# A transformer layer with routed experts on one Trainium2 core: opening turned in f32, and twelve more chunks of probabilities turned by DMA

## The reference, cut to what matters

```python
x = L0_attn_x                              # (2, 2048, 256) f32
xn = _layernorm(x, axis=-1)
# attention, one head, no key projection
scores = einsum('bqe,bke->bqk', xn @ W_qk, xn) / sqrt(256)
scores += (kpos - qpos) * alibi_slope[0]   # then the causal mask
s = einsum('bqk,bkd->bqd', softmax(scores), xn @ W_v.T)
# 8 experts, top-1 routing, capacity 512 tokens each
probs = softmax(xn @ Wr); eidx = argmax(probs)
h = maximum(xe @ W1, 0.0); ye = (h @ W2) * p_tok
x = x + s * silu(scatter(ye))
```

## Time and profile before

| what | value |
|---|---|
| median of 3 runs | 441.39 us (440.22 to 441.7) |
| the profiled execution | 440.56 us, of it 438.8 us span |
| PE busy | 420.2 us (96%) |
| DVE busy | 323.6 us (74%) |
| ACT busy | 221.7 us (51%) |
| POOL busy | 231.0 us (53%) |
| chain that ended last | PE 73%, DVE 13%, DMA 5%, ACT 4% |

### The profile page before, as it was taken

How to read it: one execution, slowest core, us unless ns; L and a number is a source line. 1 busy time by engine, 2 the same in 40 slices (tenths; PEclk the granted TensorE clock), 3 DMA queues, 4 the chain that set the end, 5 groups by cost and what they waited for, 6 DMA issues and landing times.

```text
span 438.8 us, 8377 instructions
## 1 busy us (share of the span) xinstructions
PE 420.2 (96%) x3022; PEld 287.7 (66%) x3022; DVE 323.6 (74%) x839; ACT 221.7 (51%) x436; POOL 231.0 (53%) x360
## 2 busy tenths in 40 slices
PE   5799899997999899999999999999999999999996
PEld 2367576675678677676766666666666666665676
DVE  5989778988898568778758797979696966424563
ACT  1756365353655246645435554545454545454551
POOL 5337870834726735146202666575757575757530
PEclk9999999999999999999999999999999999999999
DMA  7992749465955643266746577676778773244850
GB/s 235 357 374 68 218 133 226 94 127 109 298 149 98 103 165 71 77 229 170 143 48 253 183 232 240 196 261 184 264 174 266 178 202 92 93 119 115 154 104 30
DMA packets 99928, 74.96 MB, mean 171 GB/s; under 512 B 68911, under 2 KB 93756, under 8 KB 97840
## 3 DMA queue, kind: packets, MB, share of 16 engines
q1 hardware_dynamic: 88624, 52.06, 45.6%
q0 software_dynamic: 5824, 16.74, 12.7%
q10 hardware_dynamic: 5440, 5.64, 4.0%
HBM read 31.33 MB, written 28.58 MB: 137 GB/s over the span
## 4 chain that ended last, share of the span: by engine, by line
PE 73%; DVE 13%; DMA 5%; ACT 4%; issue 3%; POOL 0%; another core or an unknown queue 0%; ACTq 0%; SPq 0%; DVEq 0%
PE bank L1350 19%; PE bank L1352 19%; PE bank L1351 19%; PE bank L1439 4%; PE bank L1442 4%; PE bank L1441 4%; DMA pT<-p_rows 4%; DVE sc L975 3%; PE bank L1420 3%; DVE p_rows L996 2%; ACT sc L1224 2%; DVE stats L823 1%; DMA xg<-in_x 1%; DVE pT L996 1%; DVE w_l L1047 1%
## 5 line engine op out<-in xcount | busy, mean ns | idle before, releaser
L1439 PE MATMUL bank<-v_h,pT 128*128 128x257 f16 x272 | 74.6, 274 | 3.3 <-DMA pT<-p_rows 3.2
L1442 PE MATMUL bank<-v_h,pT 128*128 128x257 f16 x272 | 74.1, 272 | 0.0
L1441 PE MATMUL bank<-v_l,pT 128*128 128x256 f16 x272 | 73.7, 271 | 0.0
L1251 ACT ACTIVATE hid_h<-bank 128x512 f16<-128x512 f32 x64 | 38.0, 594 | 67.2 <-PE bank L1352 61.3
L1065 DVE SCALAR_TENSOR_TENSOR hid_l<-bank,hid_h 128x512 f16<-128x512 f32 x64 | 43.9, 685 | 37.8 <-ACT hid_h L1251 35.4
L1351 PE MATMUL bank<-w_l,hid_h 128*128 128x256 f16 x256 | 69.8, 273 | 0.0
L1350 PE MATMUL bank<-w_h,hid_h 128*128 128x256 f16 x256 | 69.8, 273 | 0.0
L1352 PE MATMUL bank<-w_h,hid_l 128*128 128x256 f16 x256 | 69.8, 273 | 0.0
L975 DVE CUSTOM_DVE_ANT_0 sc<-bank,bias,score_mul 128x512 f32<-128x512 f32 (+2 forms) x80 | 52.9, 664 | 9.6 <-PE bank L1352 9.3
L1350 PE MATMUL bank<-xT,qT_h 128*128 128x512 f16 (+3 forms) x160 | 55.0, 347 | 2.7 <-DVE cmin L975 2.4
L1351 PE MATMUL bank<-xT,qT_h 128*128 128x512 f16 (+3 forms) x160 | 55.1, 347 | 0.0
(11 more groups left out here) (183 smaller groups left out, 917.1 us busy)
## 6 DMA issues: line engine op xcount, KB each, us to landing
raw<-in_w_e SPq DMA_DIRECT2D x5, 2048.0 KB
sc<-in_w_e SPq DMA_DIRECT2D x3, 2048.0 KB
slots<-empty ACTq DMA_DIRECT2D x1, 4224.0 KB, 20.1
gates<-gate SPq DMA_DIRECT2D x8, 512.0 KB
out<-xg SPq DMA_DIRECT2D x7, 512.0 KB
rows<-xg SPq DMA_DIRECT2D x7, 512.0 KB, 7.0
rows<-so SPq DMA_DIRECT2D x7, 512.0 KB
xg<-in_x SPq DMA_DIRECT2D x6, 512.0 KB, 4.9
```

The lines of the kernel that those rows point to most:

```text
L1251: a_.activation(hid_h[:, f % HB, :], sc_ps[f % 2][:, :], ACT.Relu).then_inc(h_hi, 1)
L1439: pe.matmul(pv_ps[t % 2][:, 0:D + 1], p_h, v_h[:, at, q, 0:D + 1], start=kb == 0, stop=False)
L1441: pe.matmul(pv_ps[t % 2][:, 0:D], p_h, v_l[:, at, q, :], start=False, stop=False)
L1442: last = pe.matmul(pv_ps[t % 2][:, 0:D + 1], p_l, v_h[:, at, q, 0:D + 1], start=False, stop=kb == t % NT)
```

## The change

1. The opening. The norms of groups 0 and 1 are turned by PE in f32 (8 transposes for a group), and the split into halves is made while ACT and DVE read the bank (turned_high, turned_low). The rows that POOL scatters are gotten back from xT by four DMA transposes for a group (rows_of). Group 0's inverse deviation is made by a root on ACT, a reciprocal and a refinement on DVE; half of group 1's statistics is made on ACT.
2. Loads. `slots <- empty` (4.2 MB, ACT's queue) is issued later in the opening, the first expert's weights at t = 5.
3. by_dma is true for 12 more chunks: the first of tiles 4 to 7; (20, 0), (21, 0), (22, 0), (23, 0), (23, 1), (27, 0), (31, 0) and (31, 1). There are three buffers of rows (the third lies in hid_h, which the experts use), and a semaphore for each chunk place.
4. turn(4) goes from t = 10 to 11, turn(5) from 14 to 15.

The pieces stand in the order by_dma, buffers, SP, DVE's opening, ACT's opening, PE.

```diff
         def by_dma(t, c):
-            if t in (REST - 1, TILES - 1):
+            if chunk_blocks(t, c) < GT:
                 return False
-            if chunks(t) == 4:
-                return c == 1 if t == NT - 1 else c in ((1, 2) if t < NT else (0, 1, 2))
-            return chunks(t) == 3 and c < 2
+            if t < NT:
+                return c == 1 if t == NT - 1 else c in {2: (0,), 3: (0, 1), 4: (1, 2)}.get(chunks(t), ())
+            return c in {REST - 1: (0,), TILES - 1: (0, 1)}.get(t, range(chunks(t)) if t >= NT + GT else ())
...
+        TURN_TILE = {2: 3, 3: 6, 4: 11, 5: 15, 6: 15, LATE: REST - 8}
...
-        p_rows = [sb(f"p_rows{k}", [P, GT, 2, P], F16) for k in range(2)]
+        p_rows = [sb(f"p_rows{k}", [P, GT, 2, P], F16) for k in range(NX - 1)]
+        p_rows += [hid_h[:, HB - 2:HB, :].rearrange("p f t -> p (f t)").rearrange("p (b h t) -> p b h t", b=GT, h=2)]
...
+            def rows_of(g):
+                sp.wait_ge(xT_lo, 2 * g + 2)
+                for j in range(GT):
+                    sp.dma_start_transpose(halves[g][:, j, :].rearrange("p (b d) -> p b d", d=P),
+                                           xT[:, g, j, :, :].rearrange("p b t -> p (b t)")).then_inc(rows_back[g], 16)
...
             group_in(0)
-            sp.dma_start(raw[:, :, :], w_k[0]).then_inc(w_in[1], 16)
+            rows_of(0)
...
+                if t == 1:
+                    rows_of(1)
+                if t == 5:
+                    sp.dma_start(raw[:, :, :], w_k[0]).then_inc(w_in[1], 16)
...
-                for n in (*SPLIT_TILE, LATE):
-                    if t == {5: 14, LATE: REST - 8}.get(n, SPLIT_TILE.get(n)):
+                for n in TURN_TILE:
+                    if t == TURN_TILE[n]:
                         turn(n)
...
+            def turned_low(g, h):
+                dve.wait_ge(xT_hi, 2 * g + h + 1)
+                hi, lo = tile_rows(g, h)
+                v.scalar_tensor_tensor(lo, turned_tiles(h), X_UP, hi, ALU.mult, ALU.subtract).then_inc(xT_lo, 1)
...
-            split(0)
             query_weights()
-            rear(0)
-            norm_stats(1, range(2, GT))
-            norm_var(1)
+            turned_low(0, 0)
+            turned_low(0, 1)
...
             value_weights()
             unit(0, QRY)
+            for j in range(GT):
+                normed(1, j)
             unit(0, QRY + 1)
-            for j in range(GT - 1):
-                normed(1, j)
-            split(1)
             unit(0, VAL)
+            turned_low(1, 0)
+            dve.wait_ge(masked, 1)
+            score(0, 0)
...
+            a_.activation(warm[:, 4:5], empty[:, 0:1], ACT.Sqrt)
+            roots(0)
+            mean(2)
+            square(2)
             act.wait_ge(small_scaled, 1)
             a_.activation(wqk_h[:, :, :], wsmall[:, 0], ACT.Copy, scale=small_up[:, 0:1]).then_inc(small_hi, 1)
-            split(0)
...
             unit(0, QRY + 1)
+            a_.activation(warm[:, 4:5], empty[:, 0:1], ACT.Exp)
             unit(0, VAL)
-            split(1)
+            turned_high(1, 0)
...
             def values(t, c):
                 if by_dma(t, c):
-                    i = dma_no(t, c)
-                    pe.wait_ge(pT_in[i % 2], i // 2 * 16 + 16)
+                    pe.wait_ge(pT_in[t % 2][c], landed(t, c))
...
-                        last = pe.transpose(x_ps[h][:, at:at + P], halves[g][:, j, b * P:(b + 1) * P], ident_h[:, :])
+                        last = pe.transpose(x_ps[h][:, at:at + P], xn[:, 2 * h + j, d * P:(d + 1) * P], ident[:, :])
```

More of the change, by code:

```diff
@@ L221, in layer_kernel @@
                 [xg[j // 2].rearrange("p g d -> p (g d)")[:, j % 2 * 2 * D:(j % 2 + 1) * 2 * D] for j in range(SJ)]]
-        p_rows = [sb(f"p_rows{k}", [P, GT, 2, P], F16) for k in range(2)]
-        warm = sb("warm", [P, 4])
+        p_rows = [sb(f"p_rows{k}", [P, GT, 2, P], F16) for k in range(NX - 1)]
+        p_rows += [hid_h[:, HB - 2:HB, :].rearrange("p f t -> p (f t)").rearrange("p (b h t) -> p b h t", b=GT, h=2)]
+        warm = sb("warm", [P, 5])
+        root = sb("root", [P, GT])
+        seed = [sb(f"seed{k}", [P, GT]) for k in range(2)]
+        seed_sq = sb("seed_sq", [P, GT])
+        seed_sqv = sb("seed_sqv", [P, GT])
         bank = [ctx.enter_context(nc.psum_tensor(f"bank{k}", [P, 512], F32)) for k in range(8)]
@@ L227, in layer_kernel @@
         small_turn, small_back = bank[1][0:3, 0:P], bank[6][:, 0:3]
-        x_ps = [pv_ps[h][:, :].bitcast(F16) for h in range(2)]
+        x_ps = pv_ps
         w_turn, w_back = aux[0][0:2, 0:P], aux[1][:, 0:2]
@@ L273, in layer_kernel @@
         x_turned = sem("x_turned")
-        xT_front = sem("xT_front")
-        xT_rear = sem("xT_rear")
+        root_made = sem("root_made")
+        seed_made = sem("seed_made")
+        mean_made = sem("mean_made")
+        square_made = sem("square_made")
+        xT_hi = sem("xT_hi")
+        xT_lo = sem("xT_lo")
+        rows_back = [sem(f"rows_back{k}") for k in range(2)]
         xn_hi = sem("xn_hi")
@@ L296, in layer_kernel @@
         pT_lo = sem("pT_lo")
-        pT_in = [sem(f"pT_in{k}") for k in range(2)]
+        pT_in = [[sem(f"pT_in{k}_{c}") for c in range(NG)] for k in range(2)]
         pv_full = sem("pv_full")
@@ L367, in dma_no, with landed @@
             return chunk_no(t, c) - turn_no(t, c)
+        in_rows = [(t, c) for t in range(TILES) for c in range(chunks(t)) if by_dma(t, c)]
+        def landed(t, c):
+            return sum(by_dma(k, c) for k in range(t % 2, t + 1, 2)) * 16
         def chunk_cols(t, c):
@@ L448, in piece, with var_to, tile_rows, turned_tiles @@
             return q // PIECES, slice(q % PIECES * PIECE, (q % PIECES + 1) * PIECE)
[L450 to L457, removed]
+        def var_to(g):
+            return 1 if g == 0 else g + 2
+        def tile_rows(g, h):
+            return xT[:, g, 2 * h:2 * h + 2, 0:KD, :], xT[:, g, 2 * h:2 * h + 2, KD:2 * KD, :]
+        def turned_tiles(h):
+            return x_ps[h][:, :].rearrange("p (j k t) -> p j k t", j=2, k=KD)
+        def made_to(g):
+            return g * GT + GT if g < 2 else GT + GT + g - 1
+        def rows_to(g):
+            return g - 1
         def turned_to(g):
@@ L1372, in unit @@
                     cols = slice((n - QRY) * P, (n - QRY + 1) * P)
-                    for d in range(KD):
-                        last = product(a[:, :], wqk_h[:, d, cols], wqk_l[:, d, cols],
-                                       xT[:, at, :, d, :], xT[:, at, :, KD + d, :], d == 0, d == KD - 1)
+                    for j in [slice(0, 2), slice(2, GT)] if g == 0 else [slice(0, GT)]:
+                        if g == 0 and j.start:
+                            pe.wait_ge(xT_lo, 2)
+                        for d in range(KD):
+                            last = product(a[:, j.start * P:j.stop * P], wqk_h[:, d, cols], wqk_l[:, d, cols],
+                                           xT[:, at, j, d, :], xT[:, at, j, KD + d, :], d == 0, d == KD - 1, True)
                 elif n < RANK:
@@ L1515, in _ @@
             unit(0, VAL)
-            score(0, 0)
-            unit(0, VAL + 1)
             turn_x(1, 0)
             turn_x(1, 1)
+            unit(0, VAL + 1)
+            score(0, 0)
             unit(0, VAL + 2)
```

210 lines of the change are left out of this document (114 added, 96 removed).

## The result

| | median of the runs | profiled execution | span | mean granted clock |
|---|---|---|---|---|
| before | 441.54 us (4 runs, 440.22 to 442.42) | 440.56 us | 438.8 us | 1.0 |
| after | 475.37 us (4 runs, 472.65 to 476.26) | 476.20 us | 474.3 us | 0.964 |

The changed kernel is slower: ratio 1.0756, 95% interval 1.0726 to 1.0786. The forecast was 455, with 443 to 463 as its range. The direction was right; the loss is 34 us where 14 were expected, and 475.4 lies outside the range.

The account below looks back on a forecast made before the run. The prediction took PE, busy 96% of the span, as the bound. Terms of 12.2 us back and 27.1 lost put 440.56 + 14.9 at 455.5, stated as 455 us, range 443 to 463.

Parts of the forecast that it names:

- Transposes off PE: Added DMA chunks: 12 chunks of four transposes leave PE, 0.44 us each, 5.3 us back.
- Tile 4: values(4, 0): its transpose stands behind turn(2) and group_out(2) on SP; PE stalls 10.8 us (8.8 to 12).
- (a): Rival: transposes slip past the bulk transfers, landing 3.2 us after issue, and the clock holds; 448 us, chance 0.17.
- Tile 5: values(5, 0): the 2 MB load of raw delays the transpose, landing at 61; stall 3.5 us (0 to 8).
- The clock: After the 10.8 us wait, one stretch of eight products at half clock, 1.7 us (0 to 3.4).
- Moved turns: turn(4) behind tile 11's chunks, 1.8 us back; turn(5) behind chunk_turn(15, 1), 1.4 back, 1.1 (0 to 2.5) lost.
- Tiles 20 to 23: Stalls of 2.3 us in tile 21 behind turn(7) and 1.2 in tile 22; sum 3.5 (2 to 5).
- The load of w_k[1]: Second weights: the load moves behind tile 23's chunks and is hidden by two tiles before DVE wants it; no cost.
- The opening: Up to tile 0's first score: first product 2.1 us earlier, 1.4 back; bounds 2.1 plus 0.9, or loss of 1.0.
- (b): Rival: faster, tile 4's chunk is through SP before turn(2), stalls of tiles 4 to 7 go; 435.7 us, chance 0.10.
- (c): Rival: even, low ends of the stalls meet a better opening; 440 to 443 us, chance 0.05.
- (d): Rival: no effect, SP's transposes all stay hidden and the opening eats PE's saving; given no chance of its own.

Follow-up runs that it names:

- the kernel that keeps PE at work: Changed kernel plus unused products on PE ahead of the waits for chunks (4, 0), (5, 0), (7, 0), (21, 0) and (24, 0): 468.41 us, ratio 1.0611.
- With the old chunks: New opening with the old choice of DMA chunks, turn(4) and turn(5) moved, against the kernel before: 441.15 us, ratio 0.9985.
- picked chunks: New opening, old turn places, w_k[1] load ahead of tile 23's chunks, only (20, 0), (22, 0), (23, 0), (23, 1) added: 441.87 us, ratio 0.998.
- the opening alone: Changed kernel with old DMA chunks and old places of turn(4) and turn(5); third row buffer and first weights at t = 5 kept: 439.31 us, ratio 0.9938.
- load ahead: Changed kernel with the load of w_k[1] issued at the start of t = 23, ahead of tile 23's chunks: 473.99 us, ratio 1.0718.
- the first weights behind: Changed kernel with the first load of raw issued behind chunk_turn(5, 0), not in front of it: 467.66 us, ratio 1.0549.
- without the four chunks: Changed kernel with PE's transposes back for the first chunk of tiles 4 to 7: 451.58 us, ratio 1.0221.
- all three behind: Changed kernel with turn(2), turn(3) and the first load of raw moved behind the first chunks of tiles 4, 7 and 5: 461.42 us, ratio 1.0475.

## Why the prediction was wrong in size

In short: the stalls of tiles 4, 5 and 7 were foreseen with their cause, each 0.8 to 0.9 us too short. The steps that failed are the clock (one stretch at the half level, 1.7 us, where five cost 10.4), the moved turn(4) ("nothing new is late", where DVE's wait for spread(0) costs 4.3) and the second load ("hidden", where the transpose behind it makes PE wait 3.5 us and lose 1.6 more to the clock).

**Transposes off PE.** Right in count: PE's transposes of probabilities are 104, as the prediction has it. Each chunk's 0.44 us shows where nothing else happens in the step (drift -0.44 at values(6, 1), -0.44 at values(26, 1)).

**Tile 4.** Right: a stall of 10.8 (8.8 to 12) was forecast, and PE waits 11.7. The transpose came 6.1 us after its issue and behind the writes (group_in, which waits for them, went at 49.40), as the prediction chose against rival (a).

**Tile 5.** Right: 3.5 (0 to 8) was said, PE waits 4.3. The drift is only +3.4, since the 1.27 us of waiting for DVE ahead of it is gone, as forecast. The landing was put at 61 and came at 62.73. With the load moved behind it the wait goes.

**Tiles 6 and 7.** Tile 7: 3.8 (3 to 5) was said, PE waits 4.6; tile 6 nothing, as said.

**The clock, the term that failed first.** The prediction has one stretch at the half level, 1.7 us (0 to 3.4), behind the wait of 10.8. There were five, one behind each of the five waits shown, and by the kernel that keeps PE at work they cost 2.2 in tile 4, 1.7 in tile 5, 2.5 in tile 7, 2.5 in tile 21 and 1.6 in tile 24: 10.4 us. (In the drift against the kernel before 9.1 of it shows, since the next tile's saved transposes, 0.44, fall into the same stretch in tiles 4, 5 and 21.) The opening's 3.36 us of idle PE was the nearest row: I compared only the longest stall with it, though two others in my own sum, 3.5 and 3.8, were as long. And I sized the stretch by eight products, as the warm-up has; behind the stall of tile 7 the clock is 0.50 for the whole 5.0 us window, in which half of the work is lost. The Trainium skill ("TensorE: Matmul & The Clock Gate", Part 1) says that the clock is throttled by default and that PE's activity releases it; the windows at 0.50 behind the waits, and at 1.00 where PE was kept at work, agree.

**Moved turns, the second step that failed.** "Its group is needed a whole tile later, so nothing new is late" holds for the group and not for the queue: spread(0), behind the move on SP, comes later, and DVE waits 4.58 us for it. Back was 2.0 (1.8 was said), lost 4.3. turn(5) gives 1.4 and takes 1.5 in the changed kernel, where 1.4 and 1.1 were said (by the prediction's own numbers, 143.69 + 5.2 + 2 against 150.72 - 1.4, it should have been 1.6). With the old chunks it does neither, so moving turn(5) does not by itself give the 1.4 us back.

**Tiles 20 to 23.** In sum 3.5 (2 to 5) of stall; measured +3.9 at values(21, 0) and next to nothing in tile 22, so the sum of stalls is right and its split is not: two errors that cancel, which is luck. The landing in tile 21 was put 3.2 us after its issue and PE uses it after 5.4. In the kernel with picked chunks tile 22 has 1.26, close to the 1.2 that was said.

**The load of w_k[1], the third step.** "The load of w_k[1] moves behind tile 23's chunks and is hidden by the two tiles before DVE wants it": true for the load, and it was the transpose behind it that was late. The prediction had just used this rule for tile 5, 3.5 us, and did not use it for tile 24, which costs 3.7 and 1.6 for the clock. Tile 23's two new chunks had put the load 2.4 us ahead of tile 24's transpose, for 8 us before.

**Tile 27 and the end.** 1.5 (0.5 to 3) against +0.8 in tile 27. At the end 1.0 back and 1.2 lost; measured 1.3 back with the old chunks (drift -1.3 in tiles 28 to 30 of the kernel with the opening alone), and +2.3 ahead of values(31, 0), with the transposes saved: +0.2 in all.

**The opening.** 1.4 back was said, out of 2.1; it is 2.7. The rows of the changed kernel, first product of group 0 and first score of tile 0, answer to the last two of the earlier trace rows:

```profile
12.31 0.28 PE L1428 MATMUL bank<-xT,wqk_h 128*128 128x256 f16 x1
...
21.52 0.27 PE L1428 MATMUL bank<-xT,qT_h 128*128 128x256 f16 x1
```

The first product is 2.6 us earlier (2.1 was said), and DVE, which I took for too narrow to pass it on before tile 0's first score, passes all of it on; without the new stalls 1.4 of it goes later, in tiles 8 to 15.

**The rivals.** (a), the transposes slip past the bulk, is refuted by tile 5 with and without the load. (b), faster because tile 4's chunk gets through, fails twice: SP does have turn(2) in front, and with turn(2), turn(3) and the first load behind the chunks the kernel still takes 461.4 us. (c) and (d) did not occur, though (d)'s remark on PE's arrival 0.5 us after DVE's half was the number that dooms tile 4's chunk.

The sum of what failed: clock 8.7 more than said, spread(0) 4.3, the wait behind the second load 3.7, the waits of tiles 4, 5 and 7 together 2.5 longer, against an opening 1.3 better; some 18 of the 20.6 us between the two sums. The rest is in the several smaller terms, and I did not take it further apart.

What stays open: which waits bring the half level. Their length does not tell. A wait of 2.47 us (values(23, 0), picked chunks) was followed by it and one of 2.27 us (values(23, 0), load ahead) was not. One of 1.90 us for ACT in tile 12 of the kernel with the first weights behind was followed by it, although the prediction found nothing of the sort up to 1.8 us. Waits of 3.67 us (values(24, 0) without the four chunks) and 3.80 us (values(21, 0) with all three behind) were not. The windows right behind the 1.90 us and the 3.67 us:

```profile
131.00:134.00 3.00, 3.00 (x10) 1.56 (x11) 2.04 (x5) 3.00 (x7) 2.27 (x3) 0.50 0.90 156
...
208.20:211.00 2.80, 2.80 (x26) 1.94 (x27) 1.10 (x3) 0.63 (x1) 0.74 (x2) 1.00 1.08 285
```

So that all five waits of the changed kernel cost the clock was not sure beforehand from their length, and the prediction had no row that decides it.

## What to carry to other kernels

Before moving a piece of work into a queue, list what is due behind it and in front of it on that queue; a small transfer can land as late as the bulk ahead of it (11.7 us here for 3.2), and a moved one delays what stands behind it as well. Compare the time from the producer's end to the consumer's arrival with the transfer's bare latency: 0.45 us against 3.2 can't be mended by any order. Price a stall of PE with the clock behind it: here five stalls of 27.9 us in all cost 10.4 us more, but stalls of 3.7 and 3.8 us in two other kernels cost none, so give this term a range.

## What the runs showed of the hardware that had not been expected

- The fall of the clock can come some time behind the wait. In the changed kernel values(5, 0) begins with rows of 0.28 and 0.27 us and then goes on at 0.42; in tile 24 the products of values(24, 0) still keep the full pace and the score products behind them take up to 0.63. In the wait of tile 4 the clock falls before the wait ends: it reads 1.00 up to 42.80 and 0.50 from 43.00 on. The two rows of values(5, 0) between which it falls:

```profile
63.18 0.27 PE L1520 MATMUL bank<-v_l,pT 128*128 128x256 f16 x1
63.40 0.42 PE L1518 MATMUL bank<-v_h,pT 128*128 128x257 f16 x1
```

- A DMA transpose of a 128x1024 f16 tile, whose issue holds SP 1.25 us in a quiet queue, holds it 1.7 to 2.6 us with 1 or 2 MB just ahead, and is used 5.4 to 6.1 us after its issue behind 1 MB of writes and 11.0 to 11.7 behind the 2 MB load.
